# Two chains of accumulating scatters in place of three, and the last five weight pairs spread over sixteen steps, in a decoder layer with a mixture of experts

## The reference

```python
logits = x @ gate_w.T                      # 1024 tokens, 64 experts
w, sel = top_k(softmax(logits), 8);  w = w / sum(w)
pos = rank of the token in its expert;  valid = pos < 64
xin[e, slot] = x[token]                    # 64 slots per expert
h = silu(xin @ wg) * (xin @ wu)            # 256 -> 96
out = h @ wd                               # 96 -> 256
y[token] += out[e, slot] * w               # eight experts per token
```

## Time and profile before

| | us |
|---|---|
| median of 3 runs | 370.83 |
| lowest, highest | 370.66, 375.17 |
| the profiled execution, its own time | 368.24 |
| its span (first to last instruction on the core) | 366.4 |
| busy in the span: PE, DVE, POOL, ACT | 266.3, 232.3, 164.2, 132.0 |

### The profile page before, as it was taken

One profiled execution on the slowest core, in us unless ns is written; L12 is line 12 of the kernel. 1 busy time (PEld: TensorE's weight loads), 2 busy tenths in 40 slices (PEclk: granted clock), 3 DMA queues, 4 the chain that ended last, 5 costly groups with the idle time before them and its releaser, 6 DMA issues.

```text
span 366.4 us, 5562 instructions
## 1 busy us (share of the span) xinstructions
PE 266.3 (73%) x1851; PEld 167.1 (46%) x1851; DVE 232.3 (63%) x532; ACT 132.0 (36%) x234; POOL 164.2 (45%) x167
## 2 busy tenths in 40 slices
PE   8666696899888898798979677545799999950000
PEld 4452464567556566484655455212355555420000
DVE  0927755499966899687872877601377777730792
ACT  4600275017941149630295225100044444430021
POOL 2020022400263454825545177877055788883272
PEclk9895899899999999999989999886999999995555
DMA  6898909769999222781210099998789987665981
GB/s 232 250 123 279 316 6 121 109 203 255 383 373 201 101 92 74 149 139 56 85 67 18 30 308 306 275 272 252 210 229 309 182 150 125 74 70 101 367 321 57
DMA packets 47262, 66.62 MB, mean 182 GB/s; under 512 B 5979, under 2 KB 33241, under 8 KB 47234
## 3 DMA queue, kind: packets, MB, share of 16 engines
q1 hardware_dynamic: 39120, 56.52, 56.6%
q0 software_dynamic: 7680, 9.47, 13.6%
q10 hardware_dynamic: 434, 0.27, 0.2%
HBM read 36.45 MB, written 28.75 MB: 178 GB/s over the span
## 4 chain that ended last, share of the span: by engine, by line
PE 36%; DVE 23%; SPq 14%; DMA 11%; issue 8%; ACT 5%; POOL 1%; POOLq 0%; DVEq 0%; ACTq 0%
PE M L1317 15%; SPq L379 7%; DMA early<-early 6%; PE SA L1317 5%; SPq L369 5%; DVE nmax L911 4%; PE O L1317 4%; PE SB L1317 3%; PE O L1796 3%; DMA xin_d<-att_f,idx_last 2%; DVE early L1277 2%; DVE early L1283 2%; DMA early<-acc_d 1%; ACT probs L643 1%; PE SB L1816 1%
## 5 line engine op out<-in xcount | busy, mean ns | idle before, releaser
L507 POOL DMA_INDIRECT xin_d<-row,idx_slot x48 | 47.8, 996 | 34.9 <-DVE nmax L911 13.0
L602 POOL DMA_INDIRECT acc_d<-xp_t,idx_out x32 | 49.7, 1553 | 27.9 <-DVE idx_out L1253 13.1
L1317 PE MATMUL M<-ones_sq 128*128 128x512 bf16 x115 | 32.4, 434 | 3.8 <-DVE xp L1271 2.4
L1317 PE MATMUL SA<-early 96*128 96x256 bf16 (+1 forms) x128 | 22.0, 300 | 11.7 <-DMA early<-early 6.5
L1317 PE MATMUL M<-middle 128*128 128x256 f32 (+3 forms) x144 | 27.5, 372 | 3.5 <-DVE place_val L1053 1.3
L561 POOL TENSOR_TENSOR early<-early 128x1024 f32<-128x1024 f32 x3 | 6.4, 2145 | 48.6 <-ACT early L653 48.6
L811 ACT ACTIVATE xp<-M 128x96 f32<-128x96 f32 x32 | 8.0, 251 | 55.2 <-PE M L1317 55.2
L911 DVE TENSOR_REDUCE nmax<-SA 128x4 f32<-128x1024 f32 x16 | 19.5, 1218 | 12.4 <-PE SA L1317 12.4
L1317 PEld LDWEIGHTS M<-middle 128*128 128x128 f32 (+1 forms) x144 | 19.8, 191 | 11.1 <-issue 5.9
L1317 PE MATMUL SB<-early 96*128 96x256 bf16 (+1 forms) x128 | 21.5, 295 | 3.7 <-DVE nmax L911 2.4
L1317 PE MATMUL O<-middle,early 128*128 128x256 f32 (+1 forms) x96 | 20.8, 362 | 2.5 <-DVE middle L951 2.5
(11 more groups left out here) (261 smaller groups left out, 609.0 us busy)
## 6 DMA issues: line engine op xcount, KB each, us to landing
acc_d<-zeros SPq DMA_DIRECT2D x3, 2176.0 KB, 17.2
early<-early SPq DMA_DIRECT2D x48, 128.0 KB, 5.3
early<-acc_d SPq DMA_DIRECT2D x24, 256.0 KB, 6.0
xin_d<-zeros SPq DMA_DIRECT2D x1, 5136.0 KB, 19.4
early<-wgu SPq DMA_DIRECT2D x12, 384.0 KB, 11.8
middle<-wgu SPq DMA_DIRECT2D x12, 384.0 KB, 4.5
probs<-xin_d SPq DMA_DIRECT2D x20, 160.5 KB, 3.5
gu_sb<-wgu SPq DMA_DIRECT2D x8, 384.0 KB, 7.2
```

Source lines behind the costliest of these rows:

```text
L507: nc.gpsimd.indirect_dma_start(xin_d, bass.IndirectOffsetOnAxis(ap=idx[:, t, k:k + 1], axis=0), rows[:, t, :], None, bounds_check=SLOTS - ...
L602: nc.gpsimd.indirect_dma_start(acc_d[p % CHAINS], bass.IndirectOffsetOnAxis(ap=idx_out[:, p:p + 1], axis=0), yw[:, p % YRING, :], None, bo ...
L1317: return nc.tensor.matmul(o, l, r, start=start, stop=stop)
```

## The change

The number of tables goes from three to two; each scatter now waits for the one two before it. One table less is zeroed and loaded, and a token has four partial rows in place of six, added by one addition of two to two rows and one of one to one. In the loop the five weight pairs 26 to 30 stand behind steps 3, 6, 9, 12 and 15.

```diff
-CHAINS = 3
+CHAINS = 2
...
-            behind = {2 * n: p for n, p in enumerate(range(MID_FROM + LATE_GRP + TOPK // 2 - 1, MID_TO))}
+            behind = {3 * n + 3: p for n, p in enumerate(range(MID_FROM + LATE_GRP + TOPK // 2 - 1, MID_TO))}
...
             def halves_added(t):
                 dve.wait_ge(S["gu"][t], fin_base[t] + 16 * CHAINS)
-                nc.vector.tensor_tensor(fin[:, t, 0:3], fin[:, t, 0:3], fin[:, t, 3:6], ALU.add).then_inc(S["fpair"], 1)
-
-            def thirds_added(t, c):
+                nc.vector.tensor_tensor(fin[:, t, 0:2], fin[:, t, 0:2], fin[:, t, 2:4], ALU.add).then_inc(S["fpair"], 1)
+
+            def quarters_added(t):
                 dve.wait_ge(S["fpair"], t + 1)
-                if c == 2:
-                    dve.wait_ge(S["fadd"], 2 * t + 1)
-                nc.vector.tensor_tensor(fin[:, t, 0], fin[:, t, 0], fin[:, t, c], ALU.add).then_inc(S["fadd"], 1)
+                nc.vector.tensor_tensor(fin[:, t, 0], fin[:, t, 0], fin[:, t, 1], ALU.add).then_inc(S["fadd"], 1)
 
             def row_stats(t):
-                dve.wait_ge(S["fadd"], 2 * t + 2)
+                dve.wait_ge(S["fadd"], t + 1)
...
             for i in range(TILES + 2):
                 if i < TILES:
                     halves_added(i)
-                    thirds_added(i, 1)
                 if 1 <= i <= TILES:
                     row_stats(i - 1)
                 if i < TILES:
-                    thirds_added(i, 2)
+                    quarters_added(i)
```

## The result

The changed kernel takes 384.15 us (median of 4, 381.23 to 386.14), the kernel before beside it 371.85: a ratio of 1.031, 95% interval 1.021 to 1.041. It is slower by 11.5 us by the ratio and by 12.3 by the medians. I had forecast +7.5 with a range of +1 to +16: the direction is right, the size is short by 4 to 5.

The account below looks back on a forecast made before the run. The prediction took PE to bound the loop before and the chain of scatters after. +14.0 (scatters) - 5.6 (end) - 0.9 (front) = +7.5 on 370.83 gave 378.3 us; range 372 to 387, the forecast's own 375 to 383.

Parts of the forecast that it names:

- the mechanism: Expert loop: the bound goes from PE's 2.00 us step to the chain of scatters, 2.32 to 2.42 us per scatter.
- 0.84: Scatter chain on POOL: us taken from a scatter's landing to the start of the scatter that waits for it.
- scatter 31: Last scatter of the expert loop: forecast to start at 346.3 in place of 332.31, +14.0 us, bounds +8.8 and +27.3.
- The end: Final sums after the last landing: one table less to load and add per tile, -5.6 us, between -2.7 and -6.5.
- The front: Before batch 2: less zeroing on SP's queue removes PE's wait for the copies, -0.9 us, between 0 and -1.3.
- Rival 1: Scatters in the loop: spread loads relieve them fully, landing 4.0 to 4.3 from scatter 2 on; 374.5 us, chance 0.26.
- Rival 2: Scatters beside loads: spread but not relieved, landing stays 7.7 until pair 30 is in; 391.6 us, chance 0.11.
- the forecast's upper bound: Scatter chain in the loop: landing 7.7 for the first five cycles, scatter 31 at 359.6, +27.3 us.
- Rival 3: Whole loop: with two scatters in flight each lands sooner, 3.0 in place of 3.8; not slower, 362.5 us, chance 0.05.
- Rival 4: PE in the loop: waiting, it gets the lower clock and becomes the bound again; 390 us, chance 0.05.

Follow-up runs that it names:

- e3: Kernel before, three tables and old loads, with one added wait: each scatter also waits for the landing of the one two before; ratio 1.046 to the kernel before.
- e9: Changed kernel with four buffers for scattered rows in place of six; ratio 1.040 to the kernel before, 384.89 us.
- e10: The changed kernel measured again, unedited, in a later round; ratio 1.033 to the kernel before, median 383.72 us.
- e11: Changed kernel with its five loads back behind steps 0 to 8, run again; median 383.88 us, no ratio taken.
- e4: Changed kernel without the loop's loads of pairs 26 to 30, which reuse the weight buffers of pairs 19 to 23; ratio 1.020 to the kernel before.
- e1: Changed kernel with its five loads put back behind steps 0, 2, 4, 6 and 8, two tables kept; ratio 1.028 to the kernel before.
- e7: Kernel before, three tables and their scatters, but only two transfers and two additions per tile at the end; ratio 0.979 to the kernel before.
- e6: Kernel before, three tables, with the third zeroed late, behind the rows of batch 1; ratio 1.001 to the kernel before.
- e5: Changed kernel with scatters that write plainly in place of adding; ratio 0.987 to the kernel before.
- e2: Kernel before, three tables, with only the loads spread to steps 3, 6, 9, 12 and 15; ratio 0.999 to the kernel before.

## Why the prediction was right, and where it was short

The measured 384.15 lies inside the whole range, 372 to 387, but above the 375 to 383 that I gave the forecast itself: the mechanism is right, one term is too small.

**The mechanism, as forecast.** A scatter waits for one landing and 0.84; two in flight give 4.64 per pair with nothing beside them (4.63 to 4.65 in the cycles 16 to 20 of the profile after, landings 3.8); the bound goes from PE to POOL's chain. e3 shows it with the wait alone, e9 that PE's waiting costs nothing of its own. ACT is first held at pair 10 (its eviction at 291.30 in place of 290.7), I had said 11 to 13.

**The term that was mis-sized: scatter 31, +14.0 forecast, +19.7 measured (+18.5 in e10).** Step by step from scatter 0, in the profile after:

| stretch | forecast | measured |
|---|---|---|
| scatter 0 to 2 | 6.84 | 6.89 |
| 2 to 10, loads | 22.6 | 26.0 |
| 10 to 16, row loads | 14.5 | 15.1 |
| 16 to 30, nothing | 32.5 | 34.2 |
| 30 to 31 | 1.9 | 1.9 |

The first miss is the landing time while loads run: I took 4.8, "nearer to the 4.0", and scatters 2, 4, 6 and 8 landed in 6.3, 5.2, 5.4 and 5.7, a mean of 5.65: 4 x 0.85 = 3.4. I placed it by how long a pair of weights is in flight, and took half of the time. SP's queue after has pairs 27 to 30 here:

```profile
279.48 0.48 SPq L342 DMA_DIRECT2D middle<-wgu  x1
285.49 0.42 SPq L342 DMA_DIRECT2D middle<-wgu  x1
291.51 1.49 SPq L342 DMA_DIRECT2D middle<-wgu  x1
299.41 0.43 SPq L342 DMA_DIRECT2D middle<-wgu  x1
```

The two transfers of a pair land 3.4 to 4.9 after their issue, so a pair is in flight for about 5 us of each 6, and scatters 2, 4, 6 and 8 (278.81, 285.98, 292.06 and 298.26) each had one beside them for most of their way. The first three loads come 6.0 apart, three steps of PE; the cycle of two scatters had grown to about the same, 6.1 to 7.2, so that every even scatter met one.

The second is 1.7 in the last stretch: the cycles from 20 to 22 (5.69) and from 24 to 26 (5.28) are long. The first had a landing of 4.8 (scatter 20). No load of the kernel was beside it, but the DMA view of 329 to 335 has a packet in an instruction queue that the view of 324.5 to 329 has not:

```profile
q8 instruction: 1, 0.02, 1.7%
```

The two other long landings of this quiet stretch, scatter 22 in e9 and scatter 23 in e11 (5.0 each), have such a packet beside them too. In e3, e4 and e10 one stood beside a landing of 3.8, so this is a lead and not a shown cause. In the second cycle, scatter 24 lands at 343.3 and scatter 26 starts at 344.76, 0.6 later than the 0.84; it starts late by about as much in e1, e3, e4, e9 and e10 too. What happens there is open.

**The end: -5.6 forecast, -5.8 measured**, and alone in e7. The parts shifted: the first addition came 363.22 - 359.77 = 3.45 after the last landing (I had 4.5), the second then waited 1.26 for its transfers, and from the second to the fifth they are (370.09 - 365.64) / 3 = 1.48 apart (I had 1.54).

**The front: -0.9 forecast, not shown** (e6). The wait did go, as I had said, but I took its size in one execution for a property of the kernel.

**Sum.** +19.7 - 5.8 = +13.9 by the first pair of profiles, +18.5 - 5.6 = +12.9 with e10; the ratios give +11.5 and +12.2. The two profiled executions lie further apart, 386.14 - 368.24 = 17.9: beside the 13.9, 4.0 stand in front of scatter 0 (271.92 against 267.96), and these are no cost of the change: e1, with two tables as well, has its scatter 0 at 267.92.

**The rivals.** Rival 1 (landings near 4 from scatter 2 on) is out: 5.5 while the loads ran, and 4.4 even without them (e4). Rival 2 said that the spread loads would leave the landing at 7.7. I had drawn that from the Trainium skill (DMA: Bandwidth & Descriptors, Queues, rings and completion order), which says that each DMA engine takes turns, packet by packet, between the queues for which it has work. Measured: 7.7 with a pair of weights every second step (e1), 5.5 with one every third, 4.4 with row loads alone (e4), 3.8 with nothing. So the 7.7 does not stay for as long as the loads last. These are medians of a stretch: whether the amount in the other queue counts, or only the share of the time in which something stands there, they don't separate, and so they don't contradict the page. What none of my cases had is that the spreading gains nothing in the end: over the 3.8 of the quiet stretch, 5.65 in four cycles costs 7.4, and 7.7 in two costs 7.8. I had set the forecast's upper bound by 7.7 for five cycles; with the old loads that never lasts. Rival 3 is out: landings in the quiet stretch are 3.8 with two in flight as with three. Rival 4's first half came true, the granted clock in 305 to 345 is 0.81 and 0.88 in place of 1.00; the second did not, since PE is busy 22.75 of 31 us there and the cycle between scatters 16 and 20 is the chain's own 4.64.

## What to carry to other kernels

Where k operations are in flight in a ring, the pace is (landing time + reaction) / k, here 4.64 / 2 = 2.32 against a step of 2.00, and one less in flight turns a hidden latency into the bound for every step; check this quotient against the step before taking a buffer, a table or a chain away, and take the landing time of each stretch with the transfers that run beside it, not that of the quiet one. A saving at the end (here 5.8 us) is paid once, a longer link is paid at each of 32 steps. Spreading transfers over more steps of the latency chain did not reduce what they cost here: with early loads few links met the long latency, with spread loads more links met a medium one.

## What I had not expected of the hardware

An accumulating indirect DMA costs more than a plain one at both ends: 1.55 against 0.97 us on POOL, and a cycle of two of 4.64 against 3.27 (e5). The median landing time rises with the other transfers of the stretch, 3.8, 4.0 to 4.4, 5.5, 7.7, not in one step. And the stretch in front varies by up to 4 us between executions without any edit: the first product of batch 1 starts at 70.17 before and at 73.36 after, and at 70.64 in e1 and 73.70 in e2 on one and the same chip, before anything that was changed has run.
